# A low-rank adapted projection and a top-2 mixture of experts in one kernel: the lead of the row gathers, PSUM operands in the routing, and three reorderings

## The reference, cut to what matters

```python
# x: (64, 64, 256) = 4096 rows of 256; cond: (64, 8)
h    = x @ W_base.T + b_base
h   += 2.0 * einsum('bter,eor,be->bto', einsum('btc,erc->bter', x, As), Bs, cond)   # 8 experts of rank 16

scores = softmax(h @ gate_w.T)                       # 8 experts
topk_w, topk_i = top_k(scores, 2)
topk_w = topk_w / (topk_w.sum(-1) + 1e-20) * 2.5
g = silu(einsum('td,edf->etf', h, w_gate)) * einsum('td,edf->etf', h, w_up)   # F = 352
y = einsum('te,etd->td', combine, einsum('etf,efd->etd', g, w_down))
y += silu(h @ sw_gate) * (h @ sw_up) @ sw_down       # shared expert, 704 wide
out = x + y
```

## Time and profile before

| | |
|---|---|
| median of 3 executions | 512.72 us (511.91, 512.72, 514.34) |
| the profiled execution, its own time | 512.95 us |
| its span, first to last instruction | 511.2 us |
| mean granted clock of PE | 0.993 |
| busy: PE, DVE, ACT, POOL | 494.6, 355.9, 260.4, 249.4 us |
| instructions | 10016 |

### The profile page before, as it was taken

The page is one execution under the profiler, slowest core; times in us unless marked ns, Lnnn a source line. Parts: engine busy times, 40 slices in busy tenths (PEclk is TensorE's granted clock), DMA queues, the critical chain, the costliest instruction groups (busy, mean ns, idle before and its releaser), DMA issues.

```text
span 511.2 us, 10016 instructions
## 1 busy us (share of the span) xinstructions
PE 494.6 (97%) x3071; PEld 450.4 (88%) x3072; DVE 355.9 (70%) x764; ACT 260.4 (51%) x525; POOL 249.4 (49%) x367
## 2 busy tenths in 40 slices
PE   8999998899999999999989999999999999999996
PEld 7988986688888898999889999999998899888886
DVE  2676767897988547766656676676666666468885
ACT  3467776365754344565445455555454444444422
POOL 2042336645551264676957677676666764211100
PEclk9999999999999999999989999999999999999999
DMA  7387559237313134444334444444434452499942
GB/s 228 135 270 216 167 158 318 71 118 218 85 55 70 63 92 127 117 120 124 103 82 124 116 120 113 114 124 123 113 113 104 118 110 73 123 367 311 385 163 82
DMA packets 104922, 74.54 MB, mean 146 GB/s; under 512 B 61930, under 2 KB 99828, under 8 KB 104884
## 3 DMA queue, kind: packets, MB, share of 16 engines
q1 hardware_dynamic: 95764, 55.21, 36.9%
q0 software_dynamic: 6816, 18.62, 12.3%
q10 hardware_dynamic: 2304, 0.26, 0.4%
HBM read 40.25 MB, written 20.32 MB: 118 GB/s over the span
## 4 chain that ended last, share of the span: by engine, by line
PE 76%; DVE 11%; ACT 5%; issue 4%; DMA 3%; POOL 0%; DVEq 0%; another core or an unknown queue 0%; ACTq 0%; POOLq 0%
PE bank L272 18%; PE bank L274 17%; PE bank L273 17%; PE bank L778 10%; PE bank L750 5%; PE bank L780 5%; DVE bank L1203 1%; ACT x_half L860 1%; DVE acc L1308 1%; DVE xt_l L1018 1%; ACT gt_h L936 1%; DVE x L1042 1%; DVE pos L1067 1%; DMA raw<-x_halves 1%; PE bank L568 1%
## 5 line engine op out<-in xcount | busy, mean ns | idle before, releaser
L272 PE MATMUL bank<-w_all,rt_h 128*128 x284 | 98.1, 346 | 0.0
L274 PE MATMUL bank<-w_all,rt_l 128*128 x284 | 92.2, 324 | 0.0
L273 PE MATMUL bank<-w_all,rt_h 128*128 x284 | 92.0, 324 | 0.0
L778 PE MATMUL bank<-w_all,gt_h 128*128 (+1 forms) x213 | 78.6, 399 | 0.1
L543 POOL DMA_INDIRECT y_rows<-y_sb,dst_i x71 | 72.4, 1020 | 11.3 <-POOL spare L457 10.5
L536 POOL DMA_INDIRECT rows<-x_halves,tok_i x71 | 69.2, 975 | 12.6 <-issue 3.0
L936 ACT CAST gt_h<-bank 128x512 fp32r<-128x512 f32 (+1 forms) x48 | 28.1, 586 | 90.9 <-DVE bank L1203 82.0
L272 PE MATMUL bank<-xs_h,sg_h 128*128 128x512 f32 x176 | 71.3, 405 | 0.3 <-ACT act L926 0.3
L273 PE MATMUL bank<-xs_l,sg_h 128*128 128x512 f32 x176 | 69.5, 395 | 0.0
L274 PE MATMUL bank<-xs_h,sg_l 128*128 128x512 f32 x176 | 69.2, 393 | 0.0
L952 ACT CAST gt_h<-bank 128x384 fp32r<-128x384 f32 x71 | 34.0, 479 | 61.6 <-PE bank L750 46.6
(11 more groups left out here) (179 smaller groups left out, 1158.4 us busy)
## 6 DMA issues: line engine op xcount, KB each, us to landing
pick<-y_rows SPq DMA_DIRECT2D x16, 512.0 KB, 7.8
xin<-in_x_dram SPq DMA_DIRECT2D x8, 512.0 KB, 4.6
x_halves<-x_half SPq DMA_DIRECT2D x8, 512.0 KB, 3.2
w_own<-in_L_ffn_w_gate_dram SPq DMA_DIRECT2D x8, 352.0 KB, 4.4
w_own<-in_L_ffn_w_up_dram SPq DMA_DIRECT2D x8, 352.0 KB, 4.7
y_sb<-in_x_dram SPq DMA_DIRECT2D x5, 512.0 KB, 3.4
base_rows<-y_sb SPq DMA_DIRECT2D x5, 512.0 KB, 2.8
acc<-base_rows SPq DMA_DIRECT2D x5, 512.0 KB, 7.2
```

Source lines behind the costliest of these rows:

```text
L272: pe.matmul(o, lh, rh, start=start, stop=False, skip_group_check=skip)
L273: pe.matmul(o, lh, rl, start=False, stop=False, skip_group_check=skip)
L274: return pe.matmul(o, ll, rh, start=False, stop=stop, skip_group_check=skip)
L778: pe.matmul(YE[par][:, 0:2 * D].rearrange("p (h d) -> p h d", h=2), gt_h[par][0:n, cols], both, start=(c == 0), stop=False, skip_group_che ...
```

## The change

POOL gathers six blocks ahead instead of five, and from block 6 on each gather also waits until PE has finished the up product of five blocks before. In `places()`, nb and the sum of ranks and block bases are kept in PSUM (RANK_B) instead of SBUF, and two later operations read them, and the block numbers, from there. `load_raw(1)` is asked for one place sooner, in front of `store_x1(7)`. On PE, tiles 0 and 1 of group 0 come before the second factor, and group 1's `turn_x` before tile 2; ACT's and DVE's pieces of the second factor move behind those of the hidden product. The last sum is made and stored in two pieces of one tile.

```diff
@@ -186,9 +186,9 @@
         hot = [hot0, hot1]
-        red, top_v0, top_v1, ee, nb, bend, bbase, slot_f, slot_i, part_i, blk_cmp, blk_ef = inside("g", LO + 7 * REC, [
+        red, top_v0, top_v1, ee, bend, bbase, slot_f, slot_i, part_i, blk_cmp, blk_ef = inside("g", LO + 7 * REC, [
             ("red", [P, NT], F32), ("top_v0", [P, NT], F32), ("top_v1", [P, NT], F32), ("ee", [P, E, E], F32),
-            ("nb", [P, E], F32), ("bend", [P, E], F32), ("bbase", [P, E], F32),
+            ("bend", [P, E], F32), ("bbase", [P, E], F32),
             ("slot_f", [P, TOPK, NT], F32), ("slot_i", [P, TOPK, NT], I32), ("part_i", [P, TOPK, NT], I32),
@@ -243,6 +243,8 @@
         IOTA_AT = (NT + 1) * E
+        NB_AT = IOTA_AT + P + NBLKP
+        assert NB_AT + E <= 512
         EG, EU, TB, YE = bank[0], bank[1], bank[2], bank[6:8]
@@ -359,6 +361,8 @@
                     load_raw(0, raw)
+                if i == NG - 1:
+                    load_raw(1, raw)
                 store_x1(i)
@@ -370,7 +374,6 @@
-            load_raw(1, raw)
             load_expert(2)
@@ -438,8 +441,13 @@
             store_early(4)
-            store_own(NPG + 2)
-            sp.wait_ge(s_out, 16 * (2 * (NG - NPG) + NPG))
+            last = NG - 1
+            for n, (first, end) in enumerate(((0, 2), (2, 3), (3, 4))):
+                sp.wait_ge(s_fin, 2 * last + n + 1)
+                r = last * GT
+                sp.dma_start(out_rows[r + first * P:r + end * P, :].rearrange("(t p) d -> p t d", p=P),
+                             acc[last][:, first:end, :]).then_inc(s_out, 16)
+            sp.wait_ge(s_out, 16 * (2 * (NG - NPG) + 1 + NPG))
@@ -532,6 +540,9 @@
                     pool.wait_ge(s_turn[(i - 3) % 2], 16 * ((i - 3) // 2 + 1))
+                if i >= 6:
+                    pool.wait_ge(s_U, n_up(UE + i - 5))
                 before_dma()
@@ -546,11 +557,12 @@
                 pool.wait_ge(s_x1st[i], 16 * (NG // 2))
-            for i in range(5):
+            for i in range(6):
                 gather(i)
             for i in range(NBLK):
-                if i + 5 < NBLK:
-                    gather(i + 5)
+                if i + 6 < NBLK:
+                    gather(i + 6)
                 if i == 14:
@@ -623,6 +635,10 @@
+            pe.wait_ge(s_wal, K)
+            for t in range(2):
+                main(0, t)
             pe.wait_ge(s_db, 16 * 2)
@@ -638,15 +654,15 @@
                 if i == 0:
-                    pe.wait_ge(s_wal, K)
-                for t in range(3):
-                    if i == 0 and t == 2:
-                        pe.wait_ge(s_bl, 1)
-                    main(i, t)
-                if i + 1 < NG:
-                    turn_x(i + 1)
-                if i == 0:
+                    turn_x(1)
+                    pe.wait_ge(s_bl, 1)
+                    main(0, 2)
                     pe.wait_ge(s_bg, 1)
+                else:
+                    for t in range(3):
+                        main(i, t)
+                    if i + 1 < NG:
+                        turn_x(i + 1)
                 main(i, 3)
@@ -886,10 +902,12 @@
                 sc.copy(wa_h[:, k, :], bank[2 + k][:, 0:DX]).then_inc(s_wah, 1)
-            sc.wait_ge(s_fold, K + 1)
-            sc.copy(b_h[:], bank[4][:, 0:DX]).then_inc(s_bh, 1)
-            sc.wait_ge(s_fold, K + 2)
-            sc.copy(bias[:, D:DX], bank[6][:, 4 * E:5 * E]).then_inc(s_bg, 1)
+            def second_factor():
+                sc.wait_ge(s_fold, K + 1)
+                sc.copy(b_h[:], bank[4][:, 0:DX]).then_inc(s_bh, 1)
+                sc.wait_ge(s_fold, K + 2)
+                sc.copy(bias[:, D:DX], bank[6][:, 4 * E:5 * E]).then_inc(s_bg, 1)
@@ -898,6 +916,8 @@
                 hw_high(i)
+                if i == 0:
+                    second_factor()
                 if i >= 1:
@@ -1047,8 +1067,6 @@
                                 ALU.subtract).then_inc(s_wal, 1)
-            v.wait_ge(s_bh, 1)
-            v.tensor_tensor(b_l[:], bank[4][:, 0:DX], b_h[:].bitcast(F32), ALU.subtract).then_inc(s_bl, 1)
             count = [0]
@@ -1070,6 +1088,9 @@
                 hw_low(i)
+                if i == 0:
+                    v.wait_ge(s_bh, 1)
+                    v.tensor_tensor(b_l[:], bank[4][:, 0:DX], b_h[:].bitcast(F32), ALU.subtract).then_inc(s_bl, 1)
                 if i >= 1:
@@ -1116,24 +1137,26 @@
                 v.wait_ge(s_rank, 1)
+                nb, ranks = RANK_B[:, NB_AT:NB_AT + E], RANK_B[:, 0:NT * E]
                 over = tmp[:].rearrange("p t e -> p (t e)").rearrange("p (e t) -> p e t", e=E)
...
                                            ALU.is_gt))
-                yield link(v.tensor_reduce(nb[:], over, AX.X, ALU.add))
+                yield link(v.tensor_reduce(nb, over, AX.X, ALU.add))
                 yield small(v.tensor_tensor(ee[:], upto[:],
-                                            nb[:].rearrange("p (o e) -> p o e", o=1).broadcast_to([P, E, E]), ALU.mult))
+                                            nb.rearrange("p (o e) -> p o e", o=1).broadcast_to([P, E, E]), ALU.mult))
                 yield small(v.tensor_reduce(bend[:], ee[:], AX.X, ALU.add))
-                yield small(v.tensor_tensor(bbase[:], bend[:], nb[:], ALU.subtract))
+                yield small(v.tensor_tensor(bbase[:], bend[:], nb, ALU.subtract))
                 yield small(v.tensor_scalar(bbase[:], bbase[:], float(P), None, ALU.mult))
-                yield link(v.tensor_tensor(pos[:], RANK_B[:, 0:NT * E].rearrange("p (t e) -> p t e", e=E),
+                yield link(v.tensor_tensor(ranks.rearrange("p (t e) -> p t e", e=E), ranks.rearrange("p (t e) -> p t e", e=E),
                                            bbase[:].rearrange("p (o e) -> p o e", o=1).broadcast_to([P, NT, E]),
...
                 for c in range(TOPK):
-                    yield link(v.tensor_tensor(prob[:], pos[:], hot[c][:], ALU.mult))
+                    yield link(v.tensor_tensor(prob[:], ranks.rearrange("p (t e) -> p t e", e=E), hot[c][:], ALU.mult))
                     yield link(v.tensor_reduce(slot_f[:, c, :], prob[:], AX.X, ALU.add))
@@ -1147,7 +1170,7 @@
                 yield link(v.tensor_tensor(blk_cmp[:],
-                                           iota_blk[0:1, :].rearrange("p (b o) -> p b o", o=1)
+                                           RANK_B[0:1, IOTA_AT + P:IOTA_AT + P + NBLKP].rearrange("p (b o) -> p b o", o=1)
                                            .broadcast_to([1, NBLKP, E]),
@@ -1220,8 +1243,14 @@
                         v.wait_ge(s_D, unit(j, NC - 1) + 1)
-                    rows_of = to[:, 2 * h:2 * h + 2, :].rearrange("p t d -> p (t d)")
-                    v.tensor_tensor(rows_of, Y_B[h][:, 0:2 * D], rows_of, ALU.add).then_inc(s_fin, 1)
+                    if j == NG - 1 and h == 1:
+                        for t in range(2):
+                            v.tensor_tensor(to[:, 2 + t, :], Y_B[1][:, t * D:(t + 1) * D], to[:, 2 + t, :], ALU.add
+                                            ).then_inc(s_fin, 1)
+                    else:
+                        rows_of = to[:, 2 * h:2 * h + 2, :].rearrange("p t d -> p (t d)")
+                        v.tensor_tensor(rows_of, Y_B[h][:, 0:2 * D], rows_of, ALU.add).then_inc(s_fin, 1)
```

## The result

The changed kernel took 517.61 us (median of 10 executions, 515.98 to 524.24), the kernel before beside it 513.71 (10 executions, 511.60 to 516.65): ratio 1.0074, 95% interval 1.0046 to 1.0102. The forecast was 504.5 with a range of 499.8 to 509.0, so it is wrong, in sign too. The profiled execution took 518.64 us.

A forecast was written before the change was run, and what follows sets the result against it. The prediction took PE, busy 97% of the span, as the bound. Its terms, 2.42 + 1.56 + 2.16 + 2.1 = 8.24 us, took the profiled 512.95 us to 504.7, or 504.5 from the median; range 499.8 to 509.0.

The forecast's parts named there:

- Gathers six ahead: Expert steps: a step more of lead removes late transposes, 2.1 us won (bounds 0 and 2.88); the added wait costs 0.
- double step: Expert steps, 251.65 to 262.17 us: two steps took 3.92 us too much; forecast to stay (bounds 0 and 3.92).
- Rival C: Expert steps: early transposes at the start of PE's gate product add 0.206 us a step, giving 517.9 us; chance 0.05.
- ee, the stop at 97 and the slow clock behind it: Shared stage: nb in PSUM frees ee (3.08 to 0.2 us); PE's stop goes, 2.42 us, and the slow clock, 1.56.
- Group 1's turn: Shared stage: turned rows asked for some 4.5 us sooner remove three PE waits, 2.16 us won (bounds 0 and 2.4).
- The 0.6 us "to spare": Shared stage, after PE's stop at 97: DVE's gt_l, next to be late, is ready before 96, 0.6 us to spare.
- rival A: Expert steps: the double step at 251 goes too, 3.9 us more won, giving 500.6 us; chance 0.30.
- W2: Theory of the follow-up runs, not of the prediction: TensorE's posts come late when GpSimd waits at TensorE's semaphore.

The follow-up runs named there:

- e2: The changed kernel without the hold on the up product, still six gathers ahead: 505.59 us, 0.984 of the kernel before.
- e16: The kernel before with only group 1's turned rows asked for ahead of the store of group 7: 505.28 us, 0.995 of the kernel before.
- e9: e2 plus two more small POOL additions ahead of each gather from gather 6 on: 505.13 us, 0.975 of the kernel before.
- e11: e2 plus a POOL wait for PE's down product ahead of each scatter: 533.04 us, 1.030 of the kernel before.
- e10_held_on_g5: The changed kernel with the hold asking for DVE's product of five blocks before instead of PE's up product: 504.41 us, 0.976 of the kernel before.

## Why the prediction was wrong

**The step that failed** is in "Gathers six ahead": "the new wait is released at mid-step, later by about 0.1 us and a block earlier. Behind it in POOL's queue stands scatter(i), whose y is made a step later, so it costs 0." With six ahead taken at 2.1 us, the prediction had the 70 expert steps at 241.88 - 2.1 = 239.8; they took 252.14, and these 12.4 us are the larger part of the miss; the other, 1.7 us, lies in the shared stage (4.44 for 6.14). Of the quoted step the release itself was right (2.43 us into a step where the addition stands at 2.35 without the hold), but the gather goes 0.55 us later, since the small addition that orders POOL's transfers stands behind the hold: it comes 0.21 later, and 0.33 more lie between it and the gather. And the step looked for the cost in POOL's queue. It is not there. It is in PE's posts, which come late in 41 of the 70 steps, mostly by up to 1.4 us and at most by 2.3. That the hold brings them is shown on chip A at five ahead (5.6 us, 16 late steps against 5) and for both holds at six; that it does so by the places of the three transfers is argued, not shown. The one row of before that pointed to it, a gather at 0.40 and a transpose at 0.46 with a double step behind them, I had in hand, and used it only for the stretch at 251. Rival C took it up, but laid it on T's place, which e2 clears. That its 517.9 us is near the measured 517.61 is luck: it made every step 0.206 us longer, and what came was some steps of 3.6 to 4.9 among others of 3.30.

**What held.** The sum without the hold: 8.24 us forecast, 0.9841 of 512.95 is 8.2 measured (e2_six_free on A, 5.5 to 10.8 by its interval), though not term by term: luck has a part in so close a match.
- ee, the stop at 97 and the slow clock behind it: as forecast, 3.98 us by the sum and 4.11 by PE's starts on either side. By the Trainium skill, page "SBUF — State Buffer", section "Who interferes with whom", a VectorE instruction with two SBUF inputs is held by a GpSimd one that reads SBUF; ee went from 3.08 us to 0.22 when nb moved to PSUM, so the trace agrees. One operation next to it was not free, though it has one input in SBUF: the scaling of bbase took 1.14 us (95.24) where it had taken 0.17, and ended 0.04 behind POOL's run. DVE then works without a pause until 105.46; how much of the wait at 104.65 hangs on these 0.97 us, no run parts.
- Group 1's turn: the first two waits went (0.43 and 0.80), of the third only 0.15 of 0.93. That "POOL's sums and DVE's chain keep their distance to PE" failed: ACT's first words of group 1 came 2.61 us sooner, the marks on DVE only 1.47. DVE's operation of 75.47, with both inputs in SBUF, now runs beside POOL's split of group 1 and takes 1.48 us, where it had taken 0.42 before.
- Two new waits stand at 104.65 and 115.56. PE reached the first 5.6 us sooner than before, DVE's gt_l only 3.9 sooner (103.90 for 107.83). From PE's starts in both traces, the stage won 0.55, 0.94 and 0.14 us at the three waits and 4.11 at the stop and the slow clock; it lost 0.17 at the start and 0.70 and 0.52 at the two new waits. That is 4.35, against 4.44 at the first turn of g and 6.14 forecast. The 0.6 us "to spare" held for the unit that the prediction looked at and not two units later.
- Six ahead: 2.1 forecast, about 1.86 by the two traces on D; A can't tell it from nothing. Of the 2.88 us of the earlier trace rows, e16 on D has 1.97 (48.20 less 46.23), so the rest was not the transposes' but that of late posts or other causes.
- The double step stayed on A, B, C and E, as forecast, and rival A came true on D alone. No part of the change is its cause, since e16, without the gathers' part, has no double step there either.
- The same section of the skill says that TensorE waits on no one at SBUF. PE's matmuls agree (0.16 us apart in the long step). The sentence that by it the spacing of transfers takes nothing from PE does not follow: what was late was the word that a product of PE was finished. Whether the transfers' places make it late is what stays open.

**What stays open.** Why posts come late, and why in these places. Fast on the chips with late posts were 2.67 / 1.31 / 0.01, 3.20 / 1.31 / 0.01 to 0.3 and 0.54 / 2.14 / 0.2; slow was 3.17 / 1.70 / 0.02. The changed kernel differs from e9 in steady places by 0.02 us and is slow, but the two did not run on one chip; that its hold, released by a post which may itself be late, then moves the next gather and so feeds the trouble would explain it, but no run parts this from another cause. e11 needs no such hold to be slow. The changed kernel did not run on D, so whether the hold is free there is not known. A to C and E against D may be the chip or something else of that hour; I can't tell these apart. On D the traces also hold all of PE's posts or all but two, elsewhere 21 to 99 of 283 are missing; whether that has to do with the late ones, or the recording a part in them, no run tells. And the hold alone at six ahead was never run on one chip beside the kernel without it.

## What to carry to other kernels

A producer's semaphore can be late although its work is done: compare the consumer's start with the end of the producer's last instruction, and see whether the producer itself went on, before the consumer is blamed. That nobody stands behind a wait in a queue of transfers doesn't make it free: it moves the transfers. A kernel that is tuned to 0.1 us a step should be timed with the lead and the hold apart. And a pair of kernels that differ in one thing proves it only on the same chip: two rounds of runs agreed with W2 here until one chip ran both.

## What the hardware showed that I had not expected

The same kernel took 501.22 us on D and 536.30 on E, 7% apart, where the kernel before was only 1.7% apart (507.50 and 516.07). And on one chip, C, two kernels whose steady places differ by 0.39 us in the scatter and 0.03 in the gather took 238.78 us (e9) and 265.3 (e11) for 70 steps, with posts of TensorE mostly up to 1.4 us late in e11 and its matmuls at their usual pace. What separates them besides the places is a wait for TensorE on GpSimd; on E the wait for ScalarE in its stead was no faster. Of the kernels that beat the one before, e2_six_free has the broadest ground: its places (2.67 / 1.31 / 0.01 to 0.09) were those of six runs on A, B and C, with ratios of 0.984 to 0.989. e10_held_on_g5, at 0.976, ran on C alone.
